# Attention scores from two float32r parts on alternating 64-row halves of the array, with the mask added by 64-row matmuls

## The reference, cut to what matters

```python
query = q @ w_q.T                      # 32 heads of 16
key, value = k @ w_k.T, v @ w_v.T      # 8 groups of 16, k = v = context
scores = jnp.einsum('bghnd,bgsd->bghns', query, key) / D_HEAD ** 0.5
scores = jnp.where(mask, scores, jnp.finfo(scores.dtype).min)
attention = jax.nn.softmax(scores, axis=-1)
out = jnp.einsum('bghns,bgsd->bghnd', attention, value)
```

## Time and profile before

| what | value |
|---|---|
| median of three runs | 262.46 us (261.26 to 263.61) |
| span of the profiled execution | 259.9 us |
| instructions | 4692 |
| PE (TensorE matmuls) busy | 244.6 us, 94% |
| VectorE (DVE) busy | 206.9 us, 80% |
| ScalarE (ACT) busy | 190.2 us, 73% |
| GpSimd (POOL) busy | 124.0 us, 48% |
| data moved | 27.63 MB |

### The profile page before, as it was taken

How to read it: one execution, slowest core, us unless ns; L and a number is a source line. 1 busy time by engine, 2 the same in 40 slices (tenths; PEclk the granted TensorE clock), 3 DMA queues, 4 the chain that set the end, 5 groups by cost and what they waited for, 6 DMA issues and landing times.

```text
span 259.9 us, 4692 instructions
## 1 busy us (share of the span) xinstructions
PE 244.6 (94%) x1472; PEld 120.2 (46%) x1472; DVE 206.9 (80%) x592; ACT 190.2 (73%) x317; POOL 124.0 (48%) x176
## 2 busy tenths in 40 slices
PE   8488989799999999999999999999999999998984
PEld 8443449647433343474244365434334244444431
DVE  3789676669898479767999995989888974999995
ACT  3536598659798998587698388998969988546631
POOL 7005920466332207455888662558978987100000
PEclk9959999999999999999999999999999999999999
DMA  6999962660497850004500830720000000000004
GB/s 190 358 372 358 405 267 63 142 132 4 111 316 221 153 161 3 0 1 112 74 0 0 308 140 0 153 32 1 5 0 0 3 0 0 3 1 0 3 0 161
DMA packets 9154, 27.63 MB, mean 106 GB/s; under 512 B 1514, under 2 KB 4122, under 8 KB 7882
## 3 DMA queue, kind: packets, MB, share of 16 engines
q1 hardware_dynamic: 8698, 21.63, 28.9%
q0 software_dynamic: 288, 5.70, 6.3%
q10 hardware_dynamic: 144, 0.00, 0.0%
HBM read 23.87 MB, written 3.41 MB: 105 GB/s over the span
## 4 chain that ended last, share of the span: by engine, by line
PE 71%; DVE 7%; DMA 7%; SPq 6%; ACT 6%; issue 3%; DVEq 0%; ACTq 0%
PE bank L804 12%; PE bank L831 11%; PE bank L782 10%; DMA big<-in_ctxT 7%; PE bank L807 7%; PE bank L854 5%; PE bank L872 5%; PE bank L724 4%; PE bank L714 4%; PE bank L790 4%; PE bank L760 2%; PE bank L839 1%; DVE fs L1317 1%; SPq L470 1%; PE bank L749 1%
## 5 line engine op out<-in xcount | busy, mean ns | idle before, releaser
L1252 DVE CUSTOM_DVE_ANT_0 junk<-bank,maskb 128x512 bf16<-128x512 f32 x128 | 83.8, 687 | 13.5 <-PE bank L782 12.6
L1026 ACT ACTIVATE big<-bank 128x512 f32<-128x512 f32 x128 | 75.1, 596 | 15.1 <-PE bank L804 10.8
L590 POOL TENSOR_TENSOR big<-big,product 128x512 int32<-128x512 int32 x48 | 61.6, 1285 | 33.6 <-ACT big L1026 33.2
L804 PE MATMUL bank<-qst,kst 99*128 99x512 bf16 x128 | 49.0, 383 | 0.2
L782 PE MATMUL bank<-kst,qst 96*128 96x512 bf16 x128 | 47.8, 381 | 0.6 <-DVE mx L1252 0.4
L831 PE MATMUL bank<-big,vp 128*32 128x512 f32 x256 | 30.6, 598 | 0.0
L807 PE MATMUL bank<-ident_b,maskb 128*128 128x512 bf16 x80 | 30.4, 380 | 0.0
L600 POOL TENSOR_TENSOR mx<-mx 128x4 f32<-128x4 f32 x64 | 16.0, 249 | 22.0 <-DVE mx L1252 19.6
L782 PEld LDWEIGHTS bank<-kst,qst 96*128 96x128 bf16 x128 | 12.5, 99 | 21.4 <-issue 11.0
L804 PEld LDWEIGHTS bank<-qst,kst 99*128 99x128 bf16 x128 | 12.4, 97 | 20.6 <-ACT big L1026 7.2
L1009 ACT ACTIVATE qst<-bank 3x512 bf16<-3x512 f32 x32 | 18.9, 590 | 0.9
(11 more groups left out here) (190 smaller groups left out, 413.2 us busy)
## 6 DMA issues: line engine op xcount, KB each, us to landing
stage_w<-in_w_down POOLq DMA_DIRECT2D x1, 2816.0 KB, 11.6
stage_w<-in_w_gate SPq DMA_DIRECT2D x1, 2752.0 KB, 15.7
stage_w<-in_w_up POOLq DMA_DIRECT2D x1, 2752.0 KB, 14.8
qst<-q_parts SPq DMA_DIRECT2D x18, 128.0 KB, 4.8
big<-in_ctxT SPq DMA_DIRECT2D x8, 256.0 KB, 9.8
q_parts<-parts SPq DMA_DIRECT2D x12, 128.0 KB
big<-in_ctx SPq DMA_DIRECT2D x4, 256.0 KB, 4.7
x<-in_x SPq DMA_DIRECT2D x4, 256.0 KB, 5.9
```

What stands on the lines that cost most here:

```text
L590: nc.gpsimd.tensor_tensor(p, p, keep[:, nt, KEEP_ST.index(i):KEEP_ST.index(i) + 1, :].broadcast_to([P, HG, P]), ALU.mult).then_inc(kept, 1)
L804: i = mm(o[:, :], kst[0:KM, b, g, s * P:(s + 1) * P], qst[0:KM, tile % 2, g * HG:(g + 1) * HG, :], start=True, stop=by_keep(c, s))
L1026: fn(pt[:, c % 4, s, :], o[:, :], ACT.Exp).then_inc(drain(stage), 1)
L1252: v.tensor_tensor_reduce(junk[:, j % 2, :], o[:, :], maskb[:, tb(c // NG)[1], :], 1.0, HIDE, ALU.add, ALU.max, mx[:, c % 3, 0, hh:hh + 1]) ...
```

## The change

- Query and key are each split in two float32r parts (`upper`, and value minus `upper`). Three products are kept: 48 rows, and three rows for the maximum, 51 in all (`KM`). s and t both use all 51; in s the maximum rows of the query must be zero, so SyncE loads zeros there with each query tile.
- Groups 0 to 3 lie on partitions 0 to 50, groups 4 to 7 on 64 to 114 (`place`). The chunks take the groups in the order 0, 4, 1, 5, ... (`GROUPS`), so neighbouring chunks use opposite halves. `LAG_T` is 12 and `LAG_PV` 26: t runs exactly three chunks behind s, on the other half.
- The mask is added by two matmuls of 64 rows and 256 columns (4 heads x 64 queries) on t's own half; `maskx` holds the mask with its halves exchanged, for the queries that lie on the other partitions. Two SBUF-to-SBUF DMAs make it, in a new stage `load_maskx` right behind `mask`, before which SyncE waits for `mask_ready`.
- A split is one ScalarE copy and one VectorE operation. Two stores of 256 KB replace three of 128 KB; a stack is 6 loads (and 2 of zeros for the query) in place of 3 (key) or 6 (query). `qpick` is one stage: two float32r matmuls of 512 columns, one copy.
- SyncE's first act is a wait for a memset (3 x 512 float32) that GpSimd now issues first, and a store of zeros to DRAM.
- The adapters' early buffers move from `qst` to a ternary weight buffer; `vp` is packed 24 wide in place of 32; `woT` is loaded by 8 DMAs in the new group order; `pick` is made without waiting for `vt`.

```diff
-NTERM = 6
-KS = NTERM * DH
-KM = KS + 3
+HALF = P // 2
+KM = 3 * DH + NM
+Q_ROWS = ((0, DH), (M_ROW + NM,))
+K_ROWS = ((0, M_ROW + NM), (DH,))
+GROUPS = (0, 4, 1, 5, 2, 6, 3, 7)
-LAG_T = 11
-LAG_PV = 25
+LAG_T = 12
+LAG_PV = 26
-    ("ln0q", 2), ("y0", 0, 1), ("y0", 0, 2), ("ln0r", 2), ("mask",), ("k", 1, 2), ("load_ctx", 4), ("fabs", 0, 0),
+    ("ln0q", 2), ("y0", 0, 1), ("y0", 0, 2), ("ln0r", 2), ("mask",), ("load_maskx",), ("k", 1, 2), ("load_ctx", 4), ("fabs", 0, 0),
+def place(g):
+    return g // (NG // 2) * HALF, g % (NG // 2)
-        kst = sb("kst", [P, B, NG, SK], BF16)
-        qst = sb("qst", [P, 2, NH, P], BF16)
+        kst = sb("kst", [P, B, NG // 2, SK], F32R)
+        qst = sb("qst", [P, 2, NH // 2, P], F32R)
+            sp.wait_ge(zeros_ready, 1)
+            sp.dma_start(z_dram.rearrange("p (a s) -> p a s", s=SK), zeros.broadcast_to([NM, NG // 2, SK])).then_inc(zeros_stored, 16)
+                elif kind == "load_maskx":
+                    sp.wait_ge(mask_ready, SQ // P)
+                    sp.dma_start(maskx[0:HALF, :, :], maskb[HALF:P, :, :]).then_inc(maskx_loaded, 16)
+                    sp.dma_start(maskx[HALF:P, :, :], maskb[0:HALF, :, :]).then_inc(maskx_loaded, 16)
...
-                    mm(o[:, :], qst[0:KS, tile % 2, g * HG + hh, :], kst[0:KS, tb(tile)[0], g, :], start=True,
+                    mm(o[:, :], qst[r:r + KM, tile % 2, g * HG + hh, :], kst[r:r + KM, tb(tile)[0], g, :], start=True,
                        stop=True).then_inc(fill(stage), 1)
...
-                    i = mm(o[:, :], kst[0:KM, b, g, s * P:(s + 1) * P],
-                           qst[0:KM, tile % 2, g * HG:(g + 1) * HG, :], start=True, stop=by_keep(c, s))
+                    i = mm(o[:, :], kst[r:r + KM, b, g, s * P:(s + 1) * P],
+                           qst[r:r + KM, tile % 2, g * HG:(g + 1) * HG, :], start=True, stop=by_keep(c, s))
                     if not by_keep(c, s):
-                        i = mm(o[:, :], maskb[:, nt, s * P:(s + 1) * P], ident_b[:, :, :], start=False, stop=True)
+                        oh = o[:, :].rearrange("p (h n) -> p h n", h=HG)
+                        for half in range(2):
+                            same = maskb if half * HALF == r else maskx
+                            i = mm(oh[:, :, half * HALF:(half + 1) * HALF], same[r:r + HALF, nt, s * P:(s + 1) * P],
+                                   ident_h[r:r + HALF, :, :], start=False, stop=(half == 1))
...
-                    fn(qs[:, :], o[:, :], ACT.Copy, scale=scale).then_inc(float_copied, 1)
-                    fn(parts[:, 0, :], o[:, :], ACT.Copy, scale=scale).then_inc(drain(use), 1)
-                    act.wait_ge(remainder_ready, n + 1)
-                    fn(parts[:, 1, :], qs[:, :], ACT.Copy).then_inc(part2_ready, 1)
+                    fn(parts[:, 0, :], o[:, :], ACT.Copy, scale=1.0 if kind == "ksplit" else DH ** -0.5).then_inc(upper_ready, 1)
...
-                    v.tensor_tensor(qs[:, :], qs[:, :], parts[:, 0, :], ALU.subtract).then_inc(remainder_ready, 1)
-                    dve.wait_ge(part2_ready, n + 1)
-                    v.tensor_tensor(parts[:, 2, :], qs[:, :], parts[:, 1, :], ALU.subtract).then_inc(part3_ready, 1)
+                    v.scalar_tensor_tensor(out=parts[:, 1, :], in0=o[:, :], scalar=1.0 if kind == "ksplit" else DH ** -0.5,
+                                           in1=parts[:, 0, :].bitcast(F32), op0=ALU.mult,
+                                           op1=ALU.subtract).then_inc(drain((kind[0], t)), 1)
```

More of the change, by code:

```diff
@@ L55 @@
 VW = 32
+VS = 24
 NCHUNK = NT * NG
@@ L361, in gated_blocks_kernel @@
         ld_ffn = [sem(f"ffn_loaded{w}") for w in range(3)]
-        parts_stored = [sem(f"parts_stored{i}") for i in range(3)]
+        parts_stored = [sem(f"parts_stored{i}") for i in range(2)]
+        zeros_ready = sem("zeros_ready")
+        zeros_stored = sem("zeros_stored")
+        maskx_loaded = sem("maskx_loaded")
         k_stacked = [sem(f"k_stacked{b}") for b in range(B)]
@@ L501, in _ @@
                     dram, done = (k_dram[i], k_stacked[i]) if kind == "ksplit" else (q_dram[i], q_stacked[i])
-                    for part in range(3):
+                    for part in range(2):
                         if part == 0:
+                            sp.wait_ge(upper_ready, n + 1)
+                        else:
                             wait_drained(sp, (kind[0], i))
-                        else:
-                            sp.wait_ge((part2_ready, part3_ready)[part - 1], n + 1)
@@ new lines, in _ @@
+                    for part in range(2):
+                        sp.wait_ge(parts_stored[part], 16 * (n + 1))
+                        for half in range(2):
+                            c0 = half * NG // 2 * (SK if kind == "ksplit" else HG * P)
+                            if kind == "ksplit":
+                                for r in K_ROWS[part]:
+                                    r += half * HALF
+                                    sp.dma_start(kst[r:r + DH, i, :, :].bitcast(F32), dram[part, :, c0:c0 + NG // 2 * SK]).then_inc(done, 16)
+                            else:
+                                for r in Q_ROWS[part]:
+                                    r += half * HALF
+                                    sp.dma_start(qst[r:r + DH, i % 2, h0:NH // 2, :].bitcast(F32),
+                                                 dram[part, :, c0 + h0 * P:c0 + NH * P // 2]).then_inc(done, 16)
@@ L993, in _ @@
                     act.wait_ge(ld_ffn[w], 16)
+                    if w == 1 and i == 0:
+                        wait_filled(act, ("we", KT - 1))
+                        act.wait_ge(mask_ready, SQ // P)
                     if w == 2:
@@ L1054, in _ @@
                         wait_filled(act, ("vt",))
-                        for g in range(NPICK):
-                            wait_filled(act, ("qpick", 0, g))
                     fn(gate[:, c0:c0 + n], o[:, 0:n], ACT.Relu).then_inc(drain(("g",) + stage[1:3]), 1)
```

183 lines of the change are left out of this document (86 added, 97 removed).

## The result

The changed kernel takes 311.31 us, the median of four runs (309.80 to 315.22); the kernel before took 261.86 beside it (260.84 to 263.61). The ratio is 1.188, with a 95% interval of 1.180 to 1.195: slower by 49 us, where 257.7 was forecast and 251 to 274 given as the range. The profiled execution of after spans 313.2 us, against 259.9. It is the slowest of the four (the others span 308.0 to 309.9 us, with a granted clock of 0.90 and not 0.89; the traces of x_bf16 and x_mfirst are of their slowest execution too), so 3 to 5 us of what it shows over before are its own.

A forecast was written before the change was run, and what follows sets the result against it. PE was taken to bound the loop, by a small lead. Loop -8.5 (PE 145.5 plus 8 of waits, against 162) and front +3.7 took 259.9 to 255.1; with 2.6 between span and median, 257.7, range 251 to 274.

The forecast's parts named there:

- The front, +3.7: Before the loop: later loads and a slow clock, less a stall and qpick work, +3.7 us, ends +1 and +5.5.
- landing at 41: Before the loop: ctxT 2, issued behind SyncE's mask wait, lands at 41, so PE's matmul at 36.19 starts then, +4.8 us.
- (c): Before the loop: PE stands still some 4.6 us and the clock falls to 0.50 after it, a loss of 1.6 us.
- (d): Before the loop: the 1.56 us stall at 51.71, ahead of y0, goes as the q split no longer holds ScalarE, -1.6.
- (e): Before the loop: qpick's 6 matmuls and 4 shape changes become 2 and 2, -1.1 us.
- rival D: Rival for the loop: float32r streams at half rate, loop +23, 289 us in all; chance 0.08.
- Rivals A and C: Loop: A, s and t don't run side by side, 273.8, chance 0.20; C, a pair takes a quarter more, 264.7, 0.17.
- Rival B: Loop: shape changes between 64 and 128 rows are free, loop -16, 250.2 us in all; chance 0.13.
- The chunk, -25 us: Loop on PE: overlapping s and t saves 0.77 us per chunk, over 32 chunks 25 us.
- Shape changes, +9.4: Loop on PE: changes between 64-row and 128-row matmuls rise from 92 to 191, at 0.095 each, +9.4 us.
- Waits, 8 us: Loop: PE's waits, from SyncE, GpSimd's zeroing and in-order work, take 8 us where there were 5.5.
- The signs of being wrong: Loop: s and t start 0.2 us apart, a float32r matmul is followed 0.43 later, or VectorE's waits for s vanish.

The follow-up runs named there:

- x_bf16: The changed kernel with kst, qst, parts and pick as bf16 instead of float32r: 293.85 us.
- x_mfirst: The changed kernel with m's four small matmuls issued before the s of their slot, not between its s and t: 294.12 us.
- e_maskx_late: The changed kernel with stage load_maskx moved behind load_wq in the list: 302.75 us, 8.6 less than the change.
- m1_streams: Not the kernel: nine streams of independent matmuls alone, with bf16 matmuls between them; a float32r matmul of 512 columns takes 0.23 us.
- e_mask64: The kernel before with only the mask changed, added by two 64-row matmuls of 256 columns: 277.74 us, 1.061 times before.
- x_samehalf: The changed kernel with head groups ordered 0, 4, 5, 1, 6, 2, 3, 7, so s and t mostly share a half: 328.24 us.
- e_rows96: The changed kernel with s and t as 96-row float32r matmuls in the 128-row shape and the mask as one matmul: 288.15 us, 1.101 times before.
- x_rows64: The changed kernel with s and t over all 64 rows of a half, rows 51 to 63 being zero: 304.98 us.

## Why the prediction was wrong, step by step

**The front, +3.7: direction and mechanism right, size off.** It came to +9.1. SyncE's in-order wait for the mask is the cause of most of it (e_maskx_late: 7.6 us). The step that failed is "landing at 41": the matmul came at 45.56. The mask itself was made at 37.3 (DVE's L1252 at 36.41, 0.88 long) and not at 34.7, since the whole front had moved by 3 us (the first load was issued at 2.22 us, 1.5 later than before and not 0.9); four `load_ones` DMAs took 3.10 us of SyncE where two had taken 1.65, which I had counted nowhere; the two maskx issues and that of ctx took 0.56 to 0.59 each and not 0.44, so that ctxT 2 was issued at 39.19 and not 35.6; and it took 6.4 to land, not 5.4. (c) The clock did fall with the pause, from 44 to 51. PE worked from 45.56, so 5.4 us ran at half rate: 2.7 us and not 1.6. (d) The stall ahead of y0(1) is gone, as said. (e) The two qpick matmuls are there.

**One pass of float32r: right.** 0.23 us for 512 columns; rival D is out. (The prediction read 0.86 us for a float32 matmul out of 15.4 us of busy time for 16, which is 0.96; the spacings do give 0.86, so nothing hangs on it.)

**The halves overlap: right.** 128 matmuls ran in the time of 64 (m1_streams). Rivals A and C are out as they were put: no pair takes longer by itself. Rival B is out by e_mask64.

The Trainium skill ("TensorE: Matmul & The Clock Gate", Measured speedup vs the span model) has the 3.07 times for four row tiles from which the prediction made an estimate of 0.28 us for a pair. The trace does not bear the estimate out: a pair in a dense stream took 0.23.

**The chunk, -25 us: wrong, the saving was counted too often.** The sum took three s-t pairs in every chunk, in a dense row with its masks, 96 in all. There are 54. A step whose s stands beside a mask piece starts its t 0.26 us later (141.88 and 142.14), m and the fills break others. 42 missing pairs at 0.22 are 9 us, an estimate (a few steps start s and t 0.07 apart and lose little). x_samehalf, which takes 29 more away for 11 us, agrees with the size. The working had priced a chunk as if it stood nearly alone on PE, with 4 us taken back for masks; in fact 97 stretches share 128 steps, and a pair with 128-row work on either side gains next to nothing (m1_streams). (Rival C counted 128 pairs, the forecast 96.)

**Shape changes, +9.4: count right, price right for bf16 only.** The list of after has 194 in its loop, 191 were forecast. 80 masks cost 14.8 us in e_mask64, where 160 changes at 0.095 are 15.2. But a change seems to lay the incoming weights open, and those of float32r, and of the float32 fills, take 0.19. The forecast had no term for that: I had the width of the operands in rival C, as a slower pair. Two runs give its size. x_bf16's loop is 18.9 us shorter, of which some 5 are clock (13.6 us less at half clock, at 19.1 / 51.2 per us), which leaves 14. In the other direction e_rows96 has 10.9 us more of busy time, with float32r and without the new changes of shape. So 11 to 14 us for float32r weights; how much of it lies at changes of shape and how much at other places, such as between s and m, is not shown.

The Trainium skill ("TensorE: Matmul & The Clock Gate", Weight-path perf modes) says that fast weight load needs an input type other than FP32. It does not name float32r; the rows put float32r on FP32's side, with 188 ns against 94 for bf16. The section would have pointed at the term, though it gives no time for it.

**The clock in the loop: missing altogether, the largest term.** I had it as 1.00, and PE is over 95% busy as I said (198.8 of 205.3 us), but 54.6 us of the loop ran at 0.50. With 64 rows in use instead of 51 the clock came back: 19.1 us between the two traces (x_rows64).

**Waits, 8 us: direction right, too small.** They were to grow from 5.5 to 8. PE's idle time in the loop, which is a narrower measure, grew from 0.8 to 6.5 us, so by 5.6 and not 2.5. The longest stops are for VectorE's `h` (1.6) and for ScalarE's exponentials (2.2 in all). VectorE and ScalarE were to fall to about 130 us: ScalarE did (131.6), VectorE rose from 132.8 to 135.5.

**The signs of being wrong** were chosen badly. s and t start together in the streams, VectorE's waits for s grew, and a matmul does stand 0.42 behind a float32r one (s and m), but for another reason than half rate. None of the three was a sign of the clock, and "PE over 95% busy" came true in a loop 43 us longer.

The sum for the loop, 43.5 us measured and -8.5 forecast, is 52 apart. 19 are shown for the clock (3 to 5 of them this execution's own), 11 to 14 for the weights and 3 for waits; 9 are estimated for missing pairs. 7 to 10 us remain that no run places alone; entries to the float32 fills from the 64-row shape, which x_bf16 did not touch, are a candidate that was not tried. What in the loop's mixture brings the clock down stays open in part too: the streams tie it to few rows, x_rows64 confirms that in the kernel, but x_bf16 dips where a bf16 stream of 51 rows alone does not.

## What to carry to other kernels

Before packing the array by halves, write out PE's list and count stretches, not pairs: here each stretch cost about a weight load on the way in and another on the way out, and one pair in a stretch didn't pay for it. Keep small matmuls of another shape out of a slot; moving m by one place was worth 17 us, about half of it by the clock. Ask how many array rows each matmul uses, and try the same stream with more rows (of zeros, if need be), since the clock halved here at full busy time. And never put a load that waits for a result ahead of loads that wait for nothing.

## What the runs showed of the hardware, unexpected

- The granted clock was 0.50 in streams without any gap that used few rows: float32r on 51 rows (four streams in three runs), and bf16 on 32 (one). It stayed at 1.00 with bf16 on 51 and with float32r on 56, 64, 66, 96 and 128.
- After a change of shape a matmul came later by as much as its weights take to load: 0.19 us for four-byte weights, 0.095 for bf16. Without one, float32r and bf16 mixed at 0.70 us for three. A bf16 pair on both halves between 128-row matmuls takes nearly as long as two in a row (0.42 and 0.44).
- Matmuls on the two 64-row halves overlap fully: starts 0.02 us apart, 0.23 per pair in a dense stream.
- 51.2 us less at half clock gave back 19 us of the loop, not 25.6 (x_rows64); part of that time was not PE's to lose.
